# The up product of two batches as seven block products, in a fused attention and feed-forward kernel on one core

## The reference

```
x = x + tanh(g_xattn) * attention(layernorm(x), context)        # one head, keys = 512 context rows + 512 own rows
hidden = relu( (layernorm(x) @ sign(up_weight).T) * up_scale )   # 512 x 2048 for each batch
x = x + tanh(g_ffn) * (hidden @ sign(down_weight).T) * down_scale * output_scale
```

## Time and profile before

| | |
|---|---|
| median of 3 runs | 624.03 us (623.51 to 624.07) |
| the profiled execution's own time | 622.95 us |
| its span, first to last instruction | 620.7 us |
| busy: PE, DVE, ACT, POOL | 613.2, 254.7, 177.2, 73.8 us |
| matmuls and transposes | 2850 |
| DMA moved | 34.79 MB |

### The profile page before, as it was taken

The page is one execution under the profiler, slowest core; times in us unless marked ns, Lnnn a source line. Parts: engine busy times, 40 slices in busy tenths (PEclk is TensorE's granted clock), DMA queues, the critical chain, the costliest instruction groups (busy, mean ns, idle before and its releaser), DMA issues.

```text
span 620.7 us, 6746 instructions
## 1 busy us (share of the span) xinstructions
PE 613.2 (99%) x2850; PEld 508.9 (82%) x2850; DVE 254.7 (41%) x417; ACT 177.2 (29%) x264; POOL 73.8 (12%) x52
## 2 busy tenths in 40 slices
PE   8999999999999999999999999999999999999997
PEld 7888888888888888888888888788888888888885
DVE  4345622225522235423245213543564266436334
ACT  3724311224220225211146323322213221312211
POOL 5750202001102003020003000100010001000002
PEclk9999999999999999999999999999999999999999
DMA  8750304000303000302022233100000010001001
GB/s 304 265 191 4 103 1 135 1 0 1 101 1 136 0 1 6 97 0 102 1 69 99 71 102 111 59 0 1 34 35 1 0 61 8 1 0 69 1 1 68
DMA packets 18653, 34.79 MB, mean 56 GB/s; under 512 B 4672, under 2 KB 4672, under 8 KB 18496
## 3 DMA queue, kind: packets, MB, share of 16 engines
q1 hardware_dynamic: 18624, 34.37, 16.2%
HBM read 30.16 MB, written 4.21 MB: 55 GB/s over the span
## 4 chain that ended last, share of the span: by engine, by line
PE 90%; DMA 5%; ACT 3%; DVE 2%; issue 0%; SPq 0%; ACTq 0%
PE proj L324 32%; PE score L324 19%; PE score L497 17%; PE proj L484 17%; DMA raw_w<-in_ffn_w 4%; PE turn L316 3%; PE score L427 2%; ACT weights L553 1%; DMA rows<-in_x 1%; DVE four_x L673 0%; ACT four_x L532 0%; DVE rows L881 0%; ACT four_x L536 0%; ACT probs L646 0%; DVE raw_ctx L878 0%
## 5 line engine op out<-in xcount | busy, mean ns | idle before, releaser
L484 PE MATMUL proj<-four_x,weights 128*128 128x512 f32 x512 | 127.7, 392 | 0.4 <-ACT probs L646 0.4
L497 PE MATMUL score<-weights,probsT 128*128 128x512 f32 x512 | 126.5, 389 | 0.2 <-DVE probsT L838 0.2
L497 PEld LDWEIGHTS score<-weights,probsT 128*128 128x128 f32 x512 | 96.0, 188 | 20.7 <-DVE probsT L838 0.6
L484 PEld LDWEIGHTS proj<-four_x,weights 128*128 128x128 f32 x512 | 95.1, 188 | 20.1 <-ACT weights L553 0.8
L324 PE MATMUL score<-four_x 128*128 128x512 f32 x384 | 90.0, 391 | 0.0
L324 PE MATMUL proj<-probsT,four_x 128*128 128x512 f32 x384 | 88.2, 390 | 0.0
L646 ACT ACTIVATE probs<-proj,hid_gain 128x512 f32<-128x512 f32 x64 | 43.9, 687 | 146.5 <-PE proj L484 146.5
L324 PEld LDWEIGHTS proj<-probsT,four_x 128*128 128x128 f32 x384 | 71.9, 188 | 14.9
L540 ACT ACTIVATE four_x<-proj 128x512 fp32r<-128x512 f32 x60 | 35.8, 598 | 167.6 <-PE proj L324 167.6
L324 PEld LDWEIGHTS score<-four_x 128*128 128x128 f32 x384 | 71.5, 188 | 14.6
L324 PE MATMUL proj<-four_x,weights 128*128 128x512 f32 x336 | 76.8, 389 | 0.0
(11 more groups left out here) (66 smaller groups left out, 369.9 us busy)
## 6 DMA issues: line engine op xcount, KB each, us to landing
raw_w<-in_ffn_w SPq DMA_DIRECT2D x16, 512.0 KB, 3.3
raw_ctx<-in_ctx_turned SPq DMA_DIRECT2D x4, 1024.0 KB, 6.4
raw_ctx<-in_ctx SPq DMA_DIRECT2D x4, 1024.0 KB, 5.3
result<-rows SPq DMA_DIRECT2D x16, 256.0 KB, 2.0
rows<-in_x SPq DMA_DIRECT2D x3, 1024.0 KB, 6.4
normed<-in_x_turned SPq DMA_DIRECT2D x3, 1024.0 KB, 8.0
raw_w<-row_facts SPq DMA_DIRECT2D x3, 512.0 KB, 5.3
rows<-in_x SPq DMA_DIRECT2D x4, 256.0 KB, 4.2
```

The costliest lines, as they stand in the source:

```text
L484: last = pe.matmul(proj[:, j % 2, :], signs[:, j, 0, k * P:(k + 1) * P], four_x[:, c, s, k, :], start=(k == 0 and s == HI), stop=(k == DC ...
L497: last = pe.matmul(wide(r), hid_split[:, j % HR, s, r * P:(r + 1) * P], signs[:, j, 1, :], start=(j == 0 and s == HI), stop=(j == HC - 1 a ...
```

## The change

The diff, cut to its core:

```diff
-            def up(c, j):
-                g = HC * c + j
...
-                for k in range(DC):
-                    for s in (HI, LO):
-                        last = pe.matmul(proj[:, j % 2, :], signs[:, j, 0, k * P:(k + 1) * P], four_x[:, c, s, k, :],
-                                         start=(k == 0 and s == HI), stop=(k == DC - 1 and s == LO))
-                last.then_inc(up_done, 1)
+            def up_product(g, k, bank, left, i, start, stop):
...
+                for c in range(2):
+                    for s in (HI, LO):
+                        last = pe.matmul(bank, up_ops[:, g % 2, left, c * P:(c + 1) * P], right(i)[:, s, c, :],
+                                         start=start and c == 0 and s == HI, stop=stop and c == 1 and s == LO,
+                                         skip_group_check=True)
+                last.then_inc(up_done, 1)
...
+            def up_group(pair, j):
...
+                up_product(g, AT_P1, a, A11, B11, True, True)
+                down_piece(0)
...
+                up_product(g, AT_P7, b, S3, T3, True, True)
+                down_piece(1)
...
+                up_product(g, AT_P6, c, S2, T2, True, True)
+                down_piece(2)
+                pe.wait_ge(p1_out, g + 1)
+                up_product(g, AT_P2, a, A12, B21, False, True)
+                down_piece(3)
+                pe.wait_ge(up_sums, sum_done(g, AT_P16))
+                up_product(g, AT_P5, c, S1, T1, False, True)
+                down_piece(4)
...
+                pe.wait_ge(up_sums, sum_done(g, AT_P17))
+                up_product(g, AT_P4, b, A22, T4, False, True)
+                down_piece(5)
+                pe.wait_ge(left_ready, 4 * g + 4)
+                pe.wait_ge(up_sums, sum_done(g, AT_C22))
+                up_product(g, AT_P3, c, S4, B22, False, True)
+                down_piece(6)
+                down_piece(7)
+            def left_sums(g):
+
+                a = up_ops[:, g % 2]
+                pool.wait_ge(signs_ready, HG + g + 1)
+                pool.tensor_tensor(a[:, S3], a[:, A11].bitcast(F32), a[:, A21].bitcast(F32), ALU.subtract
+                                   ).then_inc(left_ready, 1)
...
+            def sums_of_products(pair, j):
+
+                g = HG * pair + j
+                b, c = turn[:, 0, :], turn[:, 1, :]
+                c21, c12, c22 = hid0[:, (2 * j + 1) % HR, :], hid1[:, 2 * j, :], hid1[:, 2 * j + 1, :]
+                dve.wait_ge(p1_out, g + 1)
+                dve.wait_ge(up_done, product_done(g, AT_P7))
+                dve.tensor_tensor(p17, b, p1_copy, ALU.add).then_inc(up_sums, 1)
+                dve.wait_ge(up_done, product_done(g, AT_P6))
+                dve.tensor_tensor(p16, c, p1_copy, ALU.add).then_inc(up_sums, 1)
+                dve.wait_ge(up_done, product_done(g, AT_P5))
+                dve.wait_ge(up_sums, sum_done(g, AT_P17))
+                dve.tensor_tensor(c22, c, p17, ALU.add).then_inc(up_sums, 1)
+                hidden_low(2 * pair, 2 * j)
...
+                if j == 0:
+                    act.wait_ge(x_ready, 7 * (pair + 1))
+                act.activation(p1_copy, proj[:, g % 2, :], ACT.Copy).then_inc(p1_out, 1)
```

More of the change, by code:

```diff
@@ L488, in down @@
-            def down(c, j, tiles=range(RT)):
-                g = HC * c + j
-                pe.wait_ge(hid_ready, g + 1)
-                for r in tiles:
-                    if j == 0 and c == 0:
-                        pe.wait_ge(attended, RT * (BATCH - 1) + r + 1)
-                    elif j == 0:
-                        pe.wait_ge(acc_out if r % 2 else acc_scaled, 2 * (c - 1) + r // 2 + 1)
-                    for s in (HI, LO):
-                        last = pe.matmul(wide(r), hid_split[:, j % HR, s, r * P:(r + 1) * P], signs[:, j, 1, :],
-                                         start=(j == 0 and s == HI), stop=(j == HC - 1 and s == LO))
-                    last.then_inc(down_done, 1)
@@ L515, in _ @@
-            for j, r in LAST_DOWNS:
-                down(BATCH - 1, j, tiles=[r])
+            def up_product(g, k, bank, left, i, start, stop):
[5 more added lines that the diff above has]
+                last.then_inc(up_done, 1)
@@ new lines, in down @@
+            def down(c, q, r):
+                n = HC * c + q
+                if r == 0:
+                    pe.wait_ge(hid_ready, n + 1)
+                if q == 0 and c == 0:
+                    pe.wait_ge(attended, RT * (BATCH - 1) + r + 1)
+                elif q == 0:
+                    pe.wait_ge(acc_out if r % 2 else acc_scaled, 2 * (c - 1) + r // 2 + 1)
+                for s in (HI, LO):
+                    last = pe.matmul(wide(r), hid_split[:, n % HR, s, r * P:(r + 1) * P], down_signs[:, chunk_of(q), :],
+                                     start=(q == 0 and s == HI), stop=(q == HC - 1 and s == LO))
+                last.then_inc(down_done, 1)
@@ new lines, in _ @@
+            for pair in range(2):
+                for j in range(HG):
+                    up_group(pair, j)
+                for q in (HC - 2, HC - 1):
+                    for r in range(RT):
+                        down(2 * pair, q, r)
+                if pair == 0:
+                    for q in range(HC):
+                        for r in range(RT):
+                            down(1, q, r)
+                        if q == 0:
+                            pe.wait_ge(up_sums, sum_done(HG - 1, AT_C12))
+                        if q < 4:
+                            turn_block_rows(2 * RT + 2 * q)
+                            turn_block_rows(2 * RT + 2 * q + 1)
+                else:
+                    for q in range(HC - 3):
+                        for r in range(RT):
+                            down(3, q, r)
+                    for q, r in LAST_DOWNS:
+                        down(3, q, r)
```

491 lines of the change are left out of this document (361 added, 130 removed).

## The result

The changed kernel takes 617.81 us (median of 4 runs, 617.28 to 619.39) where before takes 624.05 (4 runs): a ratio of 0.9906, 95% interval 0.9887 to 0.9925. A second measurement (experiment 9) gave 618.01 against 622.93, 0.9916 (0.9894 to 0.9939); one execution of the kernel before in it, 1038.57 us at a mean granted clock of 0.557, is left out of the ratio. The changed kernel is 0.9% faster; 617.2 was predicted, in a range of 612.3 to 623.5. The profiled execution took 617.28, its span 615.5. So 1.8 us of it lie outside the span, where before it was 2.25: the executions of every kernel with the change show 1.7 to 1.9, those of the kernel before 2.2 to 2.4. The forecast has no term for this half microsecond, and no run shows what it is.

What follows compares the result with a forecast made beforehand. TensorE's number of matmuls times 0.227 us was taken as the bound. Terms of -14.5 and -0.4 against losses summed to -6.8: 616.2 from the profiled 622.95, and 617.2 us as median, range 612.3 to 623.5.

Steps and rivals of the forecast that it cites:

- Matmuls removed: FFN up product: 448 matmuls instead of 512, 64 fewer at 0.2267 us each, -14.5 us.
- Steady groups: The 14 full groups with down pieces run at TensorE's rate, 9.97 us each: cost 0.
- drawn turn of 0.89: Inside a group, TensorE to VectorE and back: 0.2 until seen plus 0.69 for the operation, hidden by matmuls between.
- Rival B: In full groups the turns do not close: each group loses 1.5 us, 21 in all, 638 us; chance 0.12.
- Seam 1: Entry into the FFN: VectorE's nine long operations and `attended` delay group 0, with GpSimd collisions; +3.9 us (1.7 to 7.8).
- Group 7: VectorE's norms, statistics and aggregates behind group 6, 4.75 us, make sums for this group late: +1.2 us.
- Seam 2: From batch 0's down product to batch 1's: accumulators drain late with no up product between; +1.0 us (0.3 to 1.8).
- batch 1: Its down product: VectorE's long operations delay low halves, 0.6 and 1.1 us at chunks 8 and 9; +1.7 (1 to 4).
- Second pair: Its seam between down products, +0.2 us; the 0.1 for the two groups without down pieces completes the term.
- The signs' wait of before: The old kernel's gap at 395.77 in the FFN goes, as signs are taken a group ahead: -0.4 us.
- Ahead of the FFN: Before the FFN: four row tiles' transposes move into the last attention batch, 1.8 us later there, missing later, net 0.
- C, the clock falls: Waits at the entry into the FFN halve TensorE's clock for some 5 us: +2.5, 619.7, still faster; chance 0.08.

Runs made afterwards that it cites:

- experiment 9: The changed kernel run again, unedited, on the same chip as later runs: 618.01 us, ratio 0.9916 to the kernel before.
- experiment 4: The changed kernel with each group's first product computed twice, 64 more matmuls: 630.57 us, ratio 1.0120 to the kernel before.
- experiment 3: The changed kernel with one product and a down piece moved ahead, so a product directly follows the one whose sum it awaits: 633.98 us.
- experiments 2: The changed kernel with GpSimd's sums of signs of groups 0 and 1 replaced by constant fills that read nothing: 614.56 us, ratio 0.9864.
- 5: The changed kernel with VectorE's sums before group 0 moved ahead of the last projection's low half, half of `attended` later: 613.72 us, ratio 0.9849.
- experiment 6: The changed kernel with VectorE's norms moved behind group 5 and aggregates behind group 7, statistics kept behind group 6: 615.70 us, ratio 0.9885.
- experiment 7: The changed kernel with one long VectorE operation per chunk in batch 1's down product, four draining operations moved to chunk 3: 616.06 us, ratio 0.9893.
- experiments 1: The kernel before, unchanged, for a second trace: 622.48 us, first weight product at 8.88.
- 8: The kernel before with its large buffers placed by number in the changed kernel's region: 623.15 us, first weight product at 9.39.
- 11: Experiment 10's kernel with GpSimd's sums of group 1 held until VectorE's seven low parts are done: 608.84 us, ratio 0.9768.
- Experiment 10: The changed kernel with all three edits of VectorE's order together (before group 0, at group 7, in batch 1's down product): 609.10 us, ratio 0.9772.

## Why the prediction was right

The forecast was 6.8 us less by its sum; 6.2 less was measured by the medians (624.05 to 617.81), 5.7 by the two profiled executions (622.95 to 617.28), 5.2 by their spans (620.7 to 615.5). The spans fell by 7.93 in the FFN and 0.1 behind it, and the start of the FFN moved 2.87 later. Point by point, in TensorE's time, with a block's ideal length taken from its matmuls at 0.2267:

- **Matmuls removed, -14.5**: right. 2786 for 2850, a group of 9.97 us, and experiment 4 puts 64 matmuls back for about 12.7 us.
- **Steady groups, 0**: right. The drawn turn of 0.89 is 0.94 in experiment 3, and the eight matmuls between, 1.81 us, hide it. Rival B, the one on the slow side, is ruled out: of 14 full groups 12 show no gap, and the two that do, 7 and 9, stand behind other work of VectorE.
- **Seam 1, +3.9**: measured 4.29 (10.64 where 28 matmuls take 6.35). The mechanism, a chain of nine long operations with GpSimd among them and `attended` behind it, is shown by experiments 2 (2.5 us by collisions) and 5 (3.9 by the order). The collisions were drawn as four of 0.6; the trace has 0.35, 0.53, 0.54 and, over the last three operations, 1.07, the same sum. The wait for P1's copy was not drawn; it ends ahead of the one for P16 and adds nothing to the length.
- **Group 7, +1.2**: the mechanism was right (experiment 6), the size small. The first down piece behind P3 starts 10.86 after the group's start instead of 9.07: 1.8. The four norms took 2.33 beside GpSimd, not 1.91, the statistics started later for it, and the restart costs 0.12.
- **Seam 2, +1.0, and batch 1, +1.7**: 2.8 together. At seam 2 there is no named wait, but 28 matmuls from 461.27 to 468.13 take 0.5 more than 28 distances, so about half of what was drawn there, and batch 1 has the rest, 2.3; between the end of group 7 and P1 of group 8 lie 39.0 us, where 144 matmuls (32.6) and the transposes of eight tiles (0.45 each, as two tiles move the next chunk from 468.13 to 468.92 and cost it 0.1) take 36.2. The waits at chunks 8 and 9 are 0.81 and 0.75, drawn 0.6 and 1.1, and experiment 7 shows them to be made by two long operations in a row.
- **Second pair, +0.3**: 1.0. From P1 of group 8 to the end lie 109.8 us for 480 matmuls, 108.8. Group 8 loses 0.4, mostly in restarts (it has no down pieces, so only four matmuls, 0.91, stand in front of the turn of 0.94) and group 9 0.55, as VectorE's drain of batch 1, two-input additions beside `left_sums`, makes P16 late. Group 9 was among those said to have no gap ("9 to 15"); here the draw forgot a collision.
- **The signs' wait of before, -0.4**: the FFN of before lost 1.05 in all against its ideal (1024 matmuls and 12 tiles at 0.48), 0.65 more than the one wait that the prediction counted.
- **Ahead of the FFN** nothing was expected but the transposes moved there. They make 1.8 of the 2.87 by which the FFN starts later. The changed kernel's first weight product came 0.81 later (9.90 against 9.09); experiments 1 and 8 leave open whether this is arrival alone. The last 0.26 has no cause shown.

The step that failed is a rival's chance. **C, the clock falls**, was given 0.08, "still faster", and 2.5 us. Its size was right (2.6 in the one trace that has it) and so was its place, but it seems to be common.

Of 22 executions of kernels with the waits of group 0 left in (the changed one, and 3, 4, 6, 7, 9), 11 have a mean granted clock of 0.994 to 0.996. Of 12 of kernels in which those waits are gone or shorter (2, 5 and 11) none is below 0.998, and of 25 of the kernel before, beside them, none is below 0.997. (Experiment 10 isn't counted: its trace gives 1.00 up to 6.6 us and 0.95 from there to the end, with matmuls 0.227 apart all the same, which can't be read as a clock. The column fails the other way too: in the first 5 us it reads 1.00 in the trace of before, where the matmuls of the earlier trace rows are about twice as far apart as later.) Only one of the 11 has a trace; that the others fell at the same place is argued from this split, not shown. The times go with it: in experiment 6 the two executions at 0.995 took 616.29 and 616.43, the two at 1.0 took 614.88 and 615.12. In experiment 7's rows the clock falls 0.8 us into a wait and rises after six microseconds of matmuls without one. "TensorE: Matmul & The Clock Gate", "What's actually happening", in the Trainium skill, says that idleness lowers the clock and activity raises it; the rows of experiment 7 agree. So about half the runs behind the median of 617.8 probably hold one to two and a half microseconds of clock.

That the median lies 0.6 from the forecast is partly luck: the losses were drawn about a microsecond too light (9.9 in the FFN's trace, 8.1 drawn, 0.65 of it balanced by what before lost), the start came a microsecond later than drawn, the time outside the span shrank by 0.45, and the changed kernel's profiled execution lies 0.5 under its median where before's lay 1.1 under.

## What to carry to other kernels

Fewer matmuls pay in full only where every result that TensorE itself waits for has other matmuls in front of it; here eight matmuls (1.81 us) stood in front of a turn of 0.94, and with them taken away the whole gain of 14.5 us was gone (16 us lost). The losses then sit at the seams, where another engine's work stands in an order that suited the old schedule: read its queue there, and put what TensorE waits for ahead of what nobody waits for yet. Here that was worth more (8.9 us) than the change it repaired (5 to 6 us).

## What the runs showed of the hardware

- GpSimd and VectorE hold each other up when both read two operands from SBUF: 1.22 us becomes 1.57 to 1.76, 0.74 becomes up to 1.72. A GpSimd fill of the same places costs VectorE nothing (experiment 2), and `attended`, with one operand in PSUM, isn't slowed. VectorE's norms, with one tensor in SBUF and the scalars of each row, are: four take 2.33 us beside two of GpSimd's sums, 1.91 before, and those sums 1.03 and 0.92.
- Two waits of TensorE, 1.42 and 1.65 us with four matmuls between, brought its clock to 1.2 GHz in one trace, for about six microseconds of a busy engine and 2.6 us of time; by the mean clocks this happens in about every second execution, and the same waits left it up in the traces of the changed kernel and of experiments 6 and 9. It did not in the traces with a single wait of 1.27 us in group 0 (experiment 2), of 1.50 in group 7, or of 2.53 followed by a shorter one of 0.78 (experiment 3).
- A wait of TensorE costs 0.12 to 0.13 us more than the gap says: the step behind it, four matmuls, takes 1.03 to 1.04 us instead of 0.91.
